# A two-layer attention and expert kernel: twelve early tiles, a slot for each hop of the tail, and half of the first weights fetched at an earlier step

## The chip, the cores and the metric

The kernel runs on one core of a Trainium2 chip. Its engines are the tensor engine (PE, matmuls; PEld loads their weights), the vector engine (DVE), ScalarE (ACT), GpSimd (POOL) and SyncE (SP, which here issues most DMAs). The metric is device time of one launch in microseconds: the median of 3 runs is 1725.58 (1724.13 to 1726.16).

## The reference, cut to what matters

32 sequences of 128 tokens, width 256, 16 heads of 16. Four residual steps follow each other; in the second and fourth each token goes to two of eight experts. `_layernorm`, `softmax` and the rest are the usual ones.

```python
x = x + tanh(g_xattn[0]) * xattn0(layernorm(x), ctx)      # W_Q, W_K, W_V, W_O with biases, softmax over all keys
x = x + tanh(g_ffn[0])   * moe0(layernorm(x))             # top 2 of 8, relu, hidden 1024, gate = softmax of two logits
x = x + tanh(g_xattn[1]) * xattn1(layernorm(x), ctx)      # no output product, causal and key mask
x = x + tanh(g_ffn[1])   * moe1(layernorm(x))             # top 2 of 8, silu(x@w_gate) * (x@w_up) @ w_down, hidden 512
```

## The kernel before, in words

Both layers have the same plan: an attention loop and then a loop over expert tiles. All matmuls are in float32r, and precision is kept by splitting each operand into a high part (rounded by ScalarE) and a low part (the rest, by the vector engine or POOL): three products stand for one (`three`, L443 to 446).

Attention runs over steps s from -8 to 127 (`pe_step`, `act_step`, `dve_step`, `pool_step`, each engine with its own list of what it does in a step). A step handles four heads of a batch; four steps are one of the 32 batches, four batches are a group g, eight groups in all. After a batch's heads come its output transposes (`ot`), output product (`op`, layer 0 alone), residual update (`xup`) and statistics. After a group's four batches come its normalised rows (`xr`), their transposes (`lt`), router logits (`lg`), selection of two experts, ranks among the tokens of each expert (`rk`), row numbers (PI) and eight scatters by POOL that put each row into a table in DRAM sorted by expert (L1525). `Part` (L113) gives the step of each of these by group.

The expert loop takes NT = 39 tiles of 256 rows of that table. A tile's rows are fetched by SP (`sp_fetch_x`, L1606), transposed on the tensor engine (`pe_turn_x`, L614), multiplied up in four quarters (`pe_up`) while the tile before is multiplied down in two halves (`pe_down`). Its weights come in four parts n = 0 to 3 (L1582): ScalarE makes the high part (`act_w`, L840), and the low part is made by POOL (n = 0 and 3) or the vector engine (n = 1 and 2) in `low_w` (L1384). The tensor engine's first quarter of tile i waits for the low part n = 0 of tile i. POOL also scatters each finished tile's result (`pool_y`).

The two loops overlap. The last steps of attention (s = 128 to 149, LAST = 150) stand among the first tiles, four to a tile: `late(i, k)` gives step 128 + 4i + k for slot k of tile i. On the tensor engine the slots stand after the second and the fourth quarter up and after each half down (in tile 0 after each quarter); on the others after the second hidden quarter, the fourth, and around the copies of weights; POOL does slot 0 before its result scatter, slot 1 after it, slots 2 and 3 after the low weights n = 0. Every engine works strictly in its written order, so an operation that waits in a slot holds all behind it. PSUM's last two banks are dealt in turn to transposes, logits, ranks and output products in the order of the tensor engine's list (`uses_bk`), each use waiting until the one two before it has been read.

The first KE = 8 tiles are known to be full once group 4 has been counted (`dve_lists_early`, steps 101 to 104). The other tiles need the final counts (`dve_lists`, from step LIST1 = 147). SP's loop over i fetches rows for tile i + 2 at its head, but those of tile KE at the end of pass i = KE - 2, after all scatters and eight pad writes (`pad`, L833) have landed; the pads are issued in the same pass.

Of the kernel before, what the change touches and what calls it, by code (L numbers as in the profile page):

```python
# [19 lines left out]
NG = B // G  # L20
# [3 lines left out]
GE, KE = 5, 8  # L24
# [104 lines left out]
FIRST, START, LAST = -8, 128, 150  # L129
LIST0, TX, LIST1 = 101, (124, 126), 147  # L130
# [14 lines left out]
def bat(s, k):  # L145
    b, m = divmod(s - k, 4)
    return b if m == 0 and 0 <= b < B else None

# [7 lines left out]
def program(nc, A):  # L156
    ctx = ExitStack()
    with ctx:  # L158
# [216 lines left out]
        def uses_step(L, s, out):  # L375
                for name, at, empty in (("xt", X0, v_xt), ("q", Q0, v_q), ("k", K0, v_k), ("v", V0, a_v)):
                    for n in range(2):
                        if (g := grp(s, at[n])) is not None:
                            out.append(((name, g, n), empty[L, g, n]))
                if L == 0 and s == 1:  # L380
                    out.append((("bo", 0), s_bov[0]))
                if L == 0 and (b := bat(s, 8)) is not None:
                    out.append((("ot", b), v_ot[b]))
                if L == 0 and (b := bat(s, 10)) is not None:
                    out.append((("op", b), v_xup[0, b]))
                for p in PARTS:
                    for t in range(2):
                        if s == p.lt[t]:
                            out.append((("lt", p.key, t), a_lt[(L,) + p.key + (t,)]))
                    if s == p.e1:  # L390
# [125 lines left out]
        def pe_step(e, w, L, s):  # L516
# [43 lines left out]
            if L == 0 and (b := bat(s, 8)) is not None:  # L560
# [5 lines left out]
            if L == 0 and (b := bat(s, 10)) is not None:  # L566
                w.wait_ge(*v_ot[b])
                w.wait_ge(*s_wl[0, 3])
                bank_free(w, L, "op", b)
                for t in range(2):  # L570
                    ins = three(e, place[0, "op", b][:, 0:D], (OT[:, b % 2, 0, t, :], OT[:, b % 2, 1, t, :]), (WR[:, 3, 0, t], WR[:, 3, 1, t]), t == 0, t == 1)
                ins.then_inc(*m_op(b))
            for p in PARTS:
# [8 lines left out]
                if s == p.e1:  # L582
# [184 lines left out]
        def act_step(e, w, L, s):  # L767
# [13 lines left out]
            if 0 <= s < NU:  # L781
                i = s
# [10 lines left out]
            if L == 0 and (b := bat(s, 8)) is not None:  # L793
# [4 lines left out]
            for p in PARTS:  # L798
                k, g, js = (L,) + p.key, p.g, p.js
                for t in range(2):  # L800
                    if s == p.lt[t]:
# [5 lines left out]
                if s == p.lt[1]:  # L807
# [183 lines left out]
        def dve_rests(e, w, L, s):  # L991
# [5 lines left out]
            if L == 0 and (b := bat(s, 8)) is not None:  # L997
# [3 lines left out]
            if L == 0 and (b := bat(s, 10)) is not None:  # L1001
# [3 lines left out]
            for p in PARTS:  # L1005
                if s == p.e1:
# [8 lines left out]
                if s == p.rk:  # L1015
# [183 lines left out]
        def dve_step(e, w, L, s):  # L1199
# [20 lines left out]
            dve_rests(e, w, L, s - 1)  # L1220
            for j in range(G):
# [21 lines left out]
            for p in PARTS:  # L1243
                k = (L,) + p.key
                if s == p.e0:
                    dve_rsqrt_start(e, w, 1, p.js).then_inc(*v_rs2(*k))
                if s in (p.e0 + 2, p.e0 + 3):
# [8 lines left out]
                    for j in (range(p.lo, mid), range(mid, p.hi))[s - p.e0 - 2]:  # L1256
                        ins = e.tensor_scalar(xr(p.g)[:, 0, j, 0:D], X[:, p.g * G + j], mv[:, 1, j, 0:1], rs[:, 1, 1, j:j + 1], ALU.subtract, ALU.mult)
                    if s == p.e0 + 3:
# [21 lines left out]
            if (b := bat(s, 12)) is not None:  # L1280
# [215 lines left out]
        def pool_step(e, w, L, s):  # L1496
# [10 lines left out]
            for p in PARTS:  # L1507
                k, g = (L,) + p.key, p.g
                if s == p.e0:
                    w.wait_ge(*v_rs2[k])  # L1510
                    rsqrt_steps(e, w, p_c, 1, p.js, (0, 1, 2)).then_inc(*p_rs2(*k))
                if s == p.e0 + (4 if g < NG - 1 else 0):
# [7 lines left out]
                for n, (z, j) in enumerate((z, j) for z in range(2) for j in range(p.lo, p.hi)):  # L1520
                    if s == p.scatter + n // 2:
# [148 lines left out]
        def sp_attention(e, w, L):  # L1670
            sp_first(e, w, L)
            for s in range(FIRST, START):
# [139 lines left out]
```

## Time and profile before

| | |
|---|---|
| median of 3 runs | 1725.58 us |
| profiled execution | 1727.66 us, span 1725.9 us |
| TensorE clock granted, mean | 0.958 of full speed |
| busy in the span | PE 91%, PEld 82%, ACT 71%, DVE 69%, POOL 48% |
| idle before PE's row transposes, for a fetch (L614) | 30.3 us |
| fetch of 512 KB weights, issue to landing | 4.9 us |
| HBM, mean | 139 GB/s |

Busy shares are averages over stages with different limits, so the stages have to be read apart: attention of layer 0 ends near 357 us and that of layer 1 near 1278 us, and each is followed by the tiles of its layer. In the rows below a number in square brackets is the idle time of the engine before the instruction, with what ended it; "issue" is a wait that the profile puts down to nothing.

### The profile page before, as it was taken

To read this page: it belongs to the slowest core of one execution; us is meant where nothing else is said; L and a number is where in the kernel's file an instruction comes from. 1 tells how busy PE (TensorE), PEld (TensorE's weight loads), DVE (VectorE), ACT (ScalarE), POOL (GpSimd) and SP (SyncE) were. 2 spreads that over 40 slices of the span, in tenths; PEclk is the share of its full clock that TensorE was granted. 3 is DMA by queue.
4 is the path that set the end of the run, shared out by engine and by line. 5 is a ranking of instruction groups with operands and counts; after the bars stand their busy time and mean duration, and the time that the engine had idled before them with its cause. 6 is when DMAs were issued, how large, how long until landed. Compare 5 with 4: busy or idle time off the path is not lost. (4 is left out here: it accounts for less than half of the span.)

```text
span 1725.9 us, 37428 instructions
## 1 busy us (share of the span) xinstructions
PE 1562.6 (91%) x12728; PEld 1419.0 (82%) x12728; DVE 1187.1 (69%) x2778; ACT 1233.7 (71%) x2854; POOL 832.5 (48%) x907
## 2 busy tenths in 40 slices
PE   7999999978859999999998999999886749999997
PEld 5788888767859999999996777777776749999996
DVE  5677777747637677777866788888766626666664
ACT  5888888856637788888863877777775527777774
POOL 4124444336445556565553113333335546777775
PEclk9999999988979999999998999999998869999998
DMA  3222222245577777777742233333244567887883
GB/s 109 54 52 74 73 74 74 54 120 175 161 205 232 225 233 227 227 234 235 223 153 79 71 82 101 104 105 103 58 123 135 147 172 198 237 228 222 231 239 97
DMA packets 208990, 256.57 MB, mean 149 GB/s; under 512 B 29555, under 2 KB 156788, under 8 KB 208800
## 3 DMA queue, kind: packets, MB, share of 16 engines
q1 hardware_dynamic: 187040, 219.53, 43.7%
q0 software_dynamic: 21120, 34.39, 7.6%
q8 instruction: 101, 1.65, 0.4%
q14 instruction: 89, 0.73, 0.1%
q10 hardware_dynamic: 640, 0.26, 0.1%
HBM read 194.54 MB, written 45.74 MB: 139 GB/s over the span
## 5 line engine op out<-in xcount | busy, mean ns | idle before, releaser
L1384 POOL TENSOR_TENSOR KXR<-U,KXR 128x1024 fp32r<-128x1024 f32 (+1 forms) x156 | 350.0, 2245 | 308.0 <-ACT KXR L840 301.3
L444 PE MATMUL ps<-QR,KXR 128*128 128x256 f32 x1248 | 368.9, 296 | 32.3 <-issue 29.9
L445 PE MATMUL ps<-QR,KXR 128*128 128x256 f32 x1248 | 360.9, 289 | 0.0
L446 PE MATMUL ps<-QR,KXR 128*128 128x256 f32 x1248 | 360.8, 289 | 0.0
L840 ACT ACTIVATE KXR<-U 128x1024 fp32r<-128x1024 f32 (+1 forms) x312 | 288.0, 947 | 78.4 <-PE ps L446 50.6
L779 ACT ACTIVATE U<-ps,mx 128x128 f32<-128x128 f32 x1024 | 298.0, 403 | 21.5 <-DVE mx L1205 21.5
L444 PEld LDWEIGHTS ps<-QR,KXR 128*128 128x128 f32 x1248 | 248.0, 199 | 34.6 <-issue 31.5
L445 PEld LDWEIGHTS ps<-QR,KXR 128*128 128x128 f32 x1248 | 248.0, 199 | 0.0
L446 PEld LDWEIGHTS ps<-QR,KXR 128*128 128x128 f32 x1248 | 247.3, 198 | 0.0
L1205 DVE TENSOR_REDUCE mx<-ps 128x4 f32<-128x512 f32 x256 | 174.3, 684 | 68.2 <-PE ps L446 35.8
L1384 DVE TENSOR_TENSOR KXR<-U,KXR 128x1024 fp32r<-128x1024 f32 (+1 forms) x156 | 173.2, 1146 | 35.1 <-ACT KXR L840 34.9
L870 ACT ACTIVATE U<-ps,b1s 128x256 f32<-128x256 f32 x312 | 130.1, 471 | 61.1 <-PE ps L446 61.0
L522 PE MATMUL ps<-cst,U 128*128 128x128 f32 x1024 | 164.0, 283 | 10.5 <-DVE U L1215 10.0
L786 ACT ACTIVATE U<-ps 128x512 f32<-128x512 f32 x256 | 166.0, 648 | 7.1 <-PE ps L522 7.0
L1525 POOL DMA_INDIRECT xs_scr<-XR,PI x112 | 111.0, 991 | 110.8 <-DVE PI L1114 82.1
L522 PEld LDWEIGHTS ps<-cst,U 128*128 128x128 f32 x1024 | 118.1, 143 | 47.8 <-issue 23.0
L1417 DVE TENSOR_TENSOR PTR<-U,PTR 128x512 fp32r<-128x512 f32 x80 | 97.1, 1244 | 79.8 <-ACT PTR L881 79.6
L444 PE MATMUL ps<-KXR,PTR 128*128 128x256 f32 x480 | 137.8, 287 | 7.8 <-POOL KXR L1384 5.4
L445 PE MATMUL ps<-KXR,PTR 128*128 128x256 f32 x480 | 137.0, 285 | 0.0
L446 PE MATMUL ps<-KXR,PTR 128*128 128x256 f32 x480 | 136.9, 285 | 0.0
L1552 POOL DMA_INDIRECT out<-U,xi x78 | 121.7, 1561 | 20.0 <-issue 19.7
L1426 DVE TENSOR_TENSOR ps<-U,ps 128x256 f32<-128x256 f32 x156 | 70.3, 450 | 88.3 <-ACT U L873 87.8
(228 smaller groups left out, 4034.2 us busy)
## 6 DMA issues: line engine op xcount, KB each, us to landing
U<-in_wpack SPq DMA_DIRECT2D x234, 512.0 KB, 4.9
U<-in_wpack SPq DMA_DIRECT2D x78, 256.0 KB, 4.4
KXR<-U SPq DMA_DIRECT2D x504, 32.0 KB
U<-xs_scr SPq DMA_DIRECT2D x39, 258.0 KB, 4.6
U<-xs_scr SPq DMA_DIRECT2D x39, 257.0 KB, 4.7
U<-in_ctx_t SPq DMA_DIRECT2D x16, 512.0 KB, 5.7
U<-ys_scr SPq DMA_DIRECT2D x32, 256.0 KB, 3.4
U<-in_L_ffn_b SPq DMA_DIRECT2D x39, 128.0 KB, 4.0
```

The source lines that it names most:

```text
L444: e.matmul(o, wh, xh, start=first, stop=False)
L445: e.matmul(o, wh, xl, start=False, stop=False)
L446: return e.matmul(o, wl, xh, start=False, stop=done)
L522: ins = e.transpose(bank[:, h * 128:(h + 1) * 128], PB[:, i % 3, h], ident)
L779: ins = e.activation(PB[:, i % 3, h], SB_[i % 3][:, h * 128:(h + 1) * 128], ACT.Exp, bias=mx[:, i % 4, h:h + 1], scale=-1.0)
L786: e.activation(PT[:, i % 3].rearrange("p h k -> p (h k)"), pt_place["p", i][:, :], ACT.Copy).then_inc(*a_pt(L, i))
L840: e.activation(w_cols(L, WH, n), w_raw(L, n), ACT.Copy).then_inc(*a_w[n](L, i))
L870: ins = e.activation(HB[:, r, f], HBK[q][:, z * 256:z * 256 + 256], ACT.Relu, bias=b1s[:, r, f:f + 1])
L1205: e.tensor_reduce(mx[:, i % 4], SB_[i % 3][:, :].rearrange("p (h k) -> p h k", h=4), AX.X, ALU.min).then_inc(*v_mx(L, i))
L1384: e.tensor_tensor(w_cols(L, WL, n), w_raw(L, n), hi, ALU.subtract).then_inc(*l_w[n](L, i))
L1525: e.indirect_dma_start(xs_d[L], bass.IndirectOffsetOnAxis(ap=PI[:, g % 2, z, j:j + 1], axis=0), xr(g)[:, z, j, 0:ROWS[L]], None).then_inc( ...
L1552: ins = e.indirect_dma_start(ys_d[1], at, yo[:, r, a, :], None, bounds_check=T - 1, oob_is_err=False, compute_op=ALU.add)
```

## The change

KE becomes 12 and LAST 162, LIST1 158; the pads move to pass KE - 3 of SP's loop. `Part` no longer has two rhythms but one table for groups 0 to 5 (the same steps as before) and one for groups 6 and 7, whose operations each get a step of their own, also apart on the engines: transposes on the tensor engine (`lt`) and the copies of their results on ScalarE (`alt`) are one step apart, logits and their copy, ranks and their copy likewise. Group 6 is normalised at steps 130 and 131 in place of 123 and 124, scattered from 146 in place of 130; group 7 is normalised at 144 and 145 in place of 139 and 140, scattered from 158 in place of 146. The output steps of batches 30 and 31 are spread by LATE_AT. ScalarE copies tile 0's first two weight parts at steps 124 and 125 in place of 124 and 126. SP fetches the rows of tiles 0 and 1 at step 112 in place of 117, and tile 0's weight parts 0 and 1 at 112 in place of 121.

```diff
-GE, KE = 5, 8
+GE, KE = 5, 12
-FIRST, START, LAST = -8, 128, 150
-LIST0, TX, LIST1 = 101, (124, 126), 147
+FIRST, START, LAST = -8, 128, 162
+LIST0, TX, LIST1 = 101, (124, 126), 158
...
-        self.e0 = 16 * g + 4 * hi + 9
-        fast = g >= NG - 2
-        self.lt = (self.e0 + 4, self.e0 + 5)
-        self.e1 = self.e0 + 6
-        (self.max, self.index, self.sel, self.gates, self.exp, self.gates2, self.rk, self.rank, self.rows, self.scatter) = (
-            self.e1 + k for k in ((1, 1, 1, 1, 1, 2, 2, 3, 3, 3) if fast else (1, 2, 2, 3, 3, 4, 3, 4, 5, 6)))
+        if g < NG - 2:
...
+        else:
+            last = g == NG - 1
+            e = START + (16 if last else 2)
+            self.start, self.root = (e - 3, e - 2) if last else (START - 7, START - 7)
+            self.x, self.tok, self.lt, self.alt, self.axr = (e, e + 1), e + (0 if last else 2), (e + 2 + 2 * (not last), e + 3 + 2 * (not last)), (e + 3 + 2 * (not last), e + 4 + 2 * (not last)), e + 5 + 2 * (not last)
+            e = self.axr + 1
+            self.lg, self.vlg, self.max, self.index, self.sel, self.gates = e, e + 1, e + 1, e + 2, e + 2, e + 3
+            self.rk, self.exp, self.gates2, self.vrk, self.rank, self.rows = e + 4, e + 4, e + 5, e + 5, e + 6, e + 7
+            self.scatter = [e + 8 + (n // 2 if last else n) for n in range(8)]
...
+AT = {"ot": 8, "a_ot": 8, "v_ot": 9, "op": 10, "xup": 11, "stats": 12}
+LATE_AT = {"ot": {30: 0, 31: 5}, "a_ot": {30: 1, 31: 6}, "v_ot": {30: 2, 31: 7}, "op": {30: 4, 31: 8}, "xup": {30: 5, 31: 9},
+           "stats": {28: 4, 29: 5, 30: 6, 31: 10}}
...
+def step(s, name):
+    for b in range(B):
+        if s == (START + LATE_AT[name][b] if b in LATE_AT[name] else 4 * b + AT[name]):
+            return b
+    return None
...
-                    if s == p.lt[t]:
+                    if s == p.alt[t]:
...
+                    if s == TX[0] + i:
+                        act_w(e, w, L, 0, i)
                     if s == TX[i]:
-                        act_w(e, w, L, 0, i)
                         act_turn_x(e, w, L, i)
...
-                if s == 117:
+                if s == 112:
                     for i in range(2):
                         sp_fetch_x(e, w, L, i)
-                if s == 121:
-                    for b in (B - 2, B - 1):
-                        w.wait_ge(*d_k[key_queue(L, b)][L, b, 7])
-                    v = sp_expert(e, w, L, 0)
-                    for n in range(4):
-                        sp_fetch(e, w, L, 0, n, v)
+                for s0, b0, n0 in ((112, B - 6, 0), (121, B - 2, 2)):
+                    if s == s0:
+                        for b in (b0, b0 + 1):
+                            w.wait_ge(*d_k[key_queue(L, b)][L, b, 7])
+                        v = sp_expert(e, w, L, 0)
+                        for n in (n0, n0 + 1):
+                            sp_fetch(e, w, L, 0, n, v)
...
-                if i == KE - 2:
+                if i == KE - 3:
                     for x in range(E):
                         pad(e, w, L, x)
```

The order in which the instructions stand on the tensor engine at the end of layer 0's attention, before: sums of a batch's heads (L512), transposes of fetched rows (cst,U at L614), probabilities (L522), group 6's rows (cst,XR), outputs (OS), output product (WR,OT) and group 6's logits (rw,U).

```order
L512 MATMUL ps<-U,VA 32x128 x8
L614 MATMUL ps<-cst,U 128x128 x4
L522 MATMUL ps<-cst,U 128x128 x4
L580 MATMUL ps<-cst,XR 128x128 x4
L522 MATMUL ps<-cst,U 128x128 x4
L547 MATMUL ps<-cst,OS 128x128 x4
```

Then, past the output product's six matmuls:

```order
L580 MATMUL ps<-cst,XR 128x128 x4
L512 MATMUL ps<-U,VA 32x128 x8
L614 MATMUL ps<-cst,U 128x128 x4
L522 MATMUL ps<-cst,U 128x128 x4
L588 MATMUL ps<-rw,U 128x8 x8
L444 MATMUL ps<-QR,KXR 128x256
```

After the change, the same place:

```order
L537 MATMUL ps<-U,VA 32x128 x8
L639 MATMUL ps<-cst,U 128x128 x4
L547 MATMUL ps<-cst,U 128x128 x8
L572 MATMUL ps<-cst,OS 128x128 x4
L469 MATMUL ps<-WR,OT 128x256
L470 MATMUL ps<-WR,OT 128x256
```

and past the output product:

```order
L471 MATMUL ps<-WR,OT 128x256
L537 MATMUL ps<-U,VA 32x128 x8
L639 MATMUL ps<-cst,U 128x128 x4
L547 MATMUL ps<-cst,U 128x128 x4
L469 MATMUL ps<-QR,KXR 128x256
```

Group 6's two sets of transposes and its logits are gone from this place, and the first product of tile 0 (QR,KXR) follows the probabilities; the logits and transposes stand in tiles 1 and 2.

On POOL, in layer 0, around the scatters of group 7 (xs_scr<-U), before: low weights n = 0 (2x512) and n = 3 (1024), results (ys_scr).

```order
L1384 TENSOR_TENSOR KXR<-U,KXR 128x2x512
L1525 DMA xs_scr<-U,PI 34816x257 x4
L1384 TENSOR_TENSOR KXR<-U,KXR 128x1024
L1525 DMA xs_scr<-U,PI 34816x257 x2
L1550 DMA ys_scr<-U,xi 8192x256 x2
L1525 DMA xs_scr<-U,PI 34816x257 x2
L1384 TENSOR_TENSOR KXR<-U,KXR 128x2x512
```

After the change:

```order
L1414 TENSOR_TENSOR KXR<-U,KXR 128x2x512
L1555 DMA xs_scr<-U,PI 34816x257 x4
L1414 TENSOR_TENSOR KXR<-U,KXR 128x1024
L1555 DMA xs_scr<-U,PI 34816x257 x2
L1580 DMA ys_scr<-U,xi 8192x256 x2
L1555 DMA xs_scr<-U,PI 34816x257 x2
L1414 TENSOR_TENSOR KXR<-U,KXR 128x2x512
```

The pattern is the same, four scatters behind one tile's low weights n = 0, then two and two around the results of the next; it stands before the low weights n = 0 of tile 9 in place of tile 6.

On SP, in layer 0, around the last pad write (xs_scr<-cst), before: what follows is biases (b1s).

```order
L832 TENSOR_LOAD pdi
L832 ISA x2
L833 ISA
L833 DMA xs_scr<-cst 128x2x257
L1576 TENSOR_LOAD tvi
L1576 ISA x2
L1587 ISA
L1587 DMA b1s<-in_wpack 128x8
```

After the change:

```order
L858 TENSOR_LOAD pdi
L858 ISA x2
L859 ISA
L859 DMA xs_scr<-cst 128x2x257
L1635 TENSOR_LOAD tvi
L1635 ISA x2
L1636 ISA
L1636 DMA U<-xs_scr 128x2x257
```

Behind the pads there now stands a fetch of rows (U<-xs_scr), that of tile 11.

## Rows read from the trace of the kernel before

**Rows 1.** Busy time by stretch: start:end, length, engines' busy us, clock, DMA.

```profile
354.00:391.00 37.00, 24.16 (x190) 21.70 (x179) 16.77 (x55) 17.36 (x38) 9.16 (x15) 0.83 0.33 108
391.00:484.00 93.00, 70.81 (x542) 69.52 (x541) 59.94 (x124) 56.03 (x96) 54.95 (x48) 0.90 0.54 164
1278.00:1305.00 27.00, 17.94 (x150) 16.05 (x139) 16.19 (x59) 15.98 (x29) 5.92 (x9) 0.85 0.28 93
1305.00:1392.00 87.00, 58.62 (x412) 56.58 (x410) 55.23 (x166) 42.09 (x88) 51.81 (x48) 0.81 0.52 149
```

**Rows 2.** Time line of PE, layer 0: start, us, line, operation, [idle before].

```profile
356.71 0.66 PE L614 MATMUL ps<-cst,U 128*128 128x128 f32 x4
362.05 1.09 PE L580 MATMUL ps<-cst,XR 128*128 128x128 f32 x4 [4.24 <-DVE OT L1000]
...
370.98 0.63 PE L614 MATMUL ps<-cst,U 128*128 128x128 f32 x4 [4.37 <-DVE X L1004]
...
391.22 1.04 PE L614 MATMUL ps<-cst,U 128*128 128x128 f32 x4
...
436.21 0.90 PE L580 MATMUL ps<-cst,U 128*128 128x128 f32 x4 [2.67 <-DVE U L1257]
...
456.87 0.58 PE L594 MATMUL ps<-SEL,cst 128*128 128x32 f32 x2 [4.37 <-DVE SEL L1042]
...
484.21 0.55 PE L444 MATMUL ps<-QR,KXR 128*128 128x256 f32 x1 [7.00 <-issue]
...
509.53 1.12 PE L614 MATMUL ps<-cst,U 128*128 128x128 f32 x4 [12.09 <-DMA U<-xs_scr]
...
523.97 0.60 PE L614 MATMUL ps<-cst,U 128*128 128x128 f32 x4
...
535.87 0.60 PE L614 MATMUL ps<-cst,U 128*128 128x128 f32 x4
...
635.01 0.60 PE L614 MATMUL ps<-cst,U 128*128 128x128 f32 x4
```

**Rows 3.** Time line of PE, layer 1.

```profile
1278.17 0.66 PE L614 MATMUL ps<-cst,U 128*128 128x128 f32 x4
...
1304.68 1.05 PE L614 MATMUL ps<-cst,U 128*128 128x128 f32 x4
...
1392.49 0.55 PE L444 MATMUL ps<-QR,KXR 128*128 128x256 f32 x1 [7.86 <-issue]
...
1428.72 0.60 PE L614 MATMUL ps<-cst,U 128*128 128x128 f32 x4
...
1437.80 0.60 PE L614 MATMUL ps<-cst,U 128*128 128x128 f32 x4
```

**Rows 4.** Time lines of ACT and DVE: undisturbed tile, then ranks.

```profile
640.62 0.63 ACT L881 ACTIVATE WR<-U 128x512 fp32r<-128x512 f32 x1
...
641.28 3.23 DVE L1417 TENSOR_TENSOR WR<-U,WR 128x512 fp32r<-128x512 f32 x1 [1.07 <-ACT WR L881]
...
645.63 2.35 DVE L1384 TENSOR_TENSOR KXR<-U,KXR 128x1024 fp32r<-128x1024 f32 x2
...
462.45 0.76 DVE L1098 TENSOR_TENSOR CR<-CR,RK 128x8 f32<-128x8 f32 x4
```

**Rows 5.** Time line of POOL around group 7's scatters, layer 0.

```profile
464.74 1.71 POOL L1525 DMA_INDIRECT xs_scr<-U,PI  x1 [10.42 <-DVE PI L1114]
...
481.76 4.66 POOL L1384 TENSOR_TENSOR KXR<-U,KXR 128x1024 fp32r<-128x1024 f32 x2
```

**Rows 6.** Time line of SP's queue; last, the page's DMA issues.

```profile
330.44 14.81 SPq L740 DMA_DIRECT2D KXR<-U  x16
...
487.14 9.55 SPq L833 DMA_DIRECT2D xs_scr<-cst  x8
...
637.46 0.38 SPq L1606 DMA_DIRECT2D U<-xs_scr  x1
...
U<-xs_scr SPq DMA_DIRECT2D x39, 257.0 KB, 4.7
```

More of the change, by code:

```diff
@@ L118, in __init__ @@
         self.js, self.bs = slice(lo, hi), slice(g * G + lo, g * G + hi)
-        self.e0 = 16 * g + 4 * hi + 9
-        fast = g >= NG - 2
-        self.lt = (self.e0 + 4, self.e0 + 5)
-        self.e1 = self.e0 + 6
-        (self.max, self.index, self.sel, self.gates, self.exp, self.gates2, self.rk, self.rank, self.rows, self.scatter) = (
-            self.e1 + k for k in ((1, 1, 1, 1, 1, 2, 2, 3, 3, 3) if fast else (1, 2, 2, 3, 3, 4, 3, 4, 5, 6)))
+        if g < NG - 2:
+            e = 16 * g + 4 * hi + 9
+            self.start, self.root, self.x, self.tok = e, e, (e + 2, e + 3), e + 4
+            self.lt, self.alt, self.axr = (e + 4, e + 5), (e + 4, e + 5), e + 5
+            self.lg, self.vlg, self.max, self.index, self.sel, self.gates = e + 6, e + 7, e + 7, e + 8, e + 8, e + 9
+            self.rk, self.exp, self.gates2, self.vrk, self.rank, self.rows = e + 9, e + 9, e + 10, e + 10, e + 10, e + 11
+            self.scatter = [e + 12 + n // 2 for n in range(8)]
+        else:
[7 more added lines that the diff above has]
+            self.scatter = [e + 8 + (n // 2 if last else n) for n in range(8)]
 PARTS = [Part(g, 0, G) for g in range(NG)]
 NU = 4 * B
-FIRST, START, LAST = -8, 128, 150
-LIST0, TX, LIST1 = 101, (124, 126), 147
 X0, Q0, K0, V0 = (6, 7), (8, 9), (0, 1), (10, 11)
@@ L381, in uses_step @@
                     out.append((("bo", 0), s_bov[0]))
-                if L == 0 and (b := bat(s, 8)) is not None:
+                if L == 0 and (b := step(s, "ot")) is not None:
                     out.append((("ot", b), v_ot[b]))
-                if L == 0 and (b := bat(s, 10)) is not None:
+                if L == 0 and (b := step(s, "op")) is not None:
                     out.append((("op", b), v_xup[0, b]))
@@ L559, in pe_step @@
                 ins.then_inc(*s_bomm(0))
-            if L == 0 and (b := bat(s, 8)) is not None:
+            if L == 0 and (b := step(s, "ot")) is not None:
                 w.wait_ge(*v_on[0, b])
@@ L565, in pe_step @@
                 ins.then_inc(*m_ot(b))
-            if L == 0 and (b := bat(s, 10)) is not None:
+            if L == 0 and (b := step(s, "op")) is not None:
                 w.wait_ge(*v_ot[b])
@@ L792, in act_step @@
                         take(e, w, L, g, n)
-            if L == 0 and (b := bat(s, 8)) is not None:
+            if L == 0 and (b := step(s, "a_ot")) is not None:
                 w.wait_ge(*m_ot[b])
@@ L996, in dve_rests, with dve_small @@
                         rest(e, w, L, g, n)
-            if L == 0 and (b := bat(s, 8)) is not None:
+        def dve_small(e, w, L, s):
+            if L == 0 and (b := step(s, "v_ot")) is not None:
                 w.wait_ge(*a_ot[b])
@@ L1000, in dve_rests @@
                 e.tensor_tensor(ol, place[0, "ot", b][:, 0:256], oh.bitcast(F32), ALU.subtract).then_inc(*v_ot(b))
-            if L == 0 and (b := bat(s, 10)) is not None:
+            if L == 0 and (b := step(s, "xup")) is not None:
                 w.wait_ge(*m_op[b])
@@ L1244, in dve_step @@
                 k = (L,) + p.key
-                if s == p.e0:
+                if s == p.start:
                     dve_rsqrt_start(e, w, 1, p.js).then_inc(*v_rs2(*k))
-                if s in (p.e0 + 2, p.e0 + 3):
+                if s in p.x:
                     w.wait_ge(*p_rs2[k])
@@ L1255, in dve_step @@
                     mid = (p.lo + p.hi) // 2
-                    for j in (range(p.lo, mid), range(mid, p.hi))[s - p.e0 - 2]:
+                    for j in (range(p.lo, mid), range(mid, p.hi))[s - p.x[0]]:
                         ins = e.tensor_scalar(xr(p.g)[:, 0, j, 0:D], X[:, p.g * G + j], mv[:, 1, j, 0:1], rs[:, 1, 1, j:j + 1], ALU.subtract, ALU.mult)
-                    if s == p.e0 + 3:
+                    if s == p.x[1]:
                         ins.then_inc(*v_xr(*k))
@@ L1279, in dve_step @@
                     dve_lists(e, w, L, n)
-            if (b := bat(s, 12)) is not None:
+            if (b := step(s, "stats")) is not None:
                 w.wait_ge(*v_xup[L, b])
@@ L1520, in pool_step @@
                 for n, (z, j) in enumerate((z, j) for z in range(2) for j in range(p.lo, p.hi)):
-                    if s == p.scatter + n // 2:
+                    if s == p.scatter[n]:
                         w.wait_ge(*v_pi[k])
```

15 lines of the change are left out of this document (8 added, 7 removed).

## The prediction

> **What bounds the kernel now.** I first read busy and granted clock by stage [rows 1], then the tensor engine's line in time through the tail of each layer [rows 2, 3], then one undisturbed tile on the two engines that feed it [rows 4], then POOL's and SP's queues [rows 5, 6]. The reader is to see four things.
>
> In undisturbed tiles the tensor engine never waits: a tile takes 11.9 us in layer 0 (523.97 to 535.87) and 9.08 in layer 1 (1428.72 to 1437.80) [rows 2, 3]. So time can only come back from the stretch around the seam, where attention ends and expert tiles begin. There the engine is busy 24.2 of 37 us, then 70.8 of 93, in layer 1 17.9 of 27, then 58.6 of 87, and its granted clock is 0.81 to 0.90 of full speed: after an idle stretch the lower level of 1.2 GHz is granted for a while, so most waits cost 1 to 2 us more than their length [rows 1]. The waits have names: 4.24 us for a bank behind the vector engine, 4.37 for a residual update, 2.67 for a normalised row, 4.37 for the selection, 7.00 before tile 6, 12.09 for the first row fetch that needs the final lists [rows 2].
>
> The 7.00 is POOL's: it issues eight scatters of the last group from 464.74, puts other work between, and only then makes the low part of tile 6's first weights (first of the two at 481.76, so about 484.1); the tensor engine starts at 484.21 [rows 2, 5]. The 12.09 is SP's: eight pad writes take 9.55 us of issuing, and the row fetch stands behind them [rows 6].
>
> **The change part by part.** I cut each layer into A (first transposes of gathered rows to the start of tile 1), B (from there to the last wait on POOL's scatters) and C (to the first undisturbed tile).
>
> *A, hops of group 6 out of attention and tile 0.* Group 6's normalisation, transposes, logits and ranks leave steps 123 to 130, and batch 30's output product leaves tile 0. Today A is 34.5 us in layer 0 (356.71 to 391.22) and 26.5 in layer 1 (1278.17 to 1304.68) [rows 2, 3]. The 4.24 us wait goes, since the vector engine no longer sits on group 5's last scatter before it frees the bank; the 4.37 goes, since half of tile 0's weights are there early and the residual update is no longer queued behind the copy of group 6's rows. What is left: busy 24.2 at clock 0.83 is about 20.1 at full clock; the 32 of 190 matmuls that leave (8 transposes, 16 logits, 6 output products, 2 ranks) are 3.8 us at 0.12 each, and 2.7 lie before the cut [rows 1, 2]. That makes 13.6, and I add 3 for steps that stay paced by ScalarE: 16.6. Layer 1: 17.9 at 0.85 is 15.2, less 26 matmuls (3.1), plus 3: 15.1 [rows 1]. Gain 17.9 and 11.4, together 29.3. The bounds are the 3 us (0 if nothing paces the steps, 9 if as much idle stays as in layer 1 today).
>
> The earlier fetch of half the weights costs SP's queue: two row fetches and two 512 KB fetches now stand between the key copies of batches 30 and 31. Those 16 copies take SP from 330.44 to 345.25 [rows 6], and the tensor engine goes on without an idle row after them. Bounds: nothing, to 4 us a layer (the 4.7 us in which a row fetch lands, less what is over when batch 31's copies are issued [rows 6]). I take 1.5 each, nearer to nothing since eight copies are issued over some 5 us: A gains 26.3 net. The Trainium skill, "DMA: Bandwidth & Descriptors", section "Queues, rings and completion order", says that on each DMA engine the descriptors of a ring are consumed in ring order; by that the keys wait for all the weights in front of them, 4 us a layer, and the sum below is 5 us less gain. No run here shows yet which.
>
> *B, a slot per hop.* A slot is reached by each engine at its own time. In a tile of layer 0 the tensor engine is at its four slots 3.3, 6.2, 9.0 and 11.9 us after the tile's start (quarters of 96 matmuls). ScalarE reaches its first at 6.2 (640.62 + 0.63 against 635.01), the vector engine at 9.5 (641.28 + 3.23), about 10.7, 11.8 and 13.0 (645.63 + 2.35) [rows 2, 4]. So a vector result from slot 0 or 1 of a tile is late for tensor slot 2, however tidy the table looks. Layer 0, by the new table: tile 1, output and transposes behind the vector engine's slots 1 and 3, 3.8 in four waits; tile 2, the output product of batch 31 at tensor slot 0 wants a bank that ScalarE frees in its own slot 0 (6.2 + 0.6 against 3.3), 3.5; tile 3, ranks behind the selection, 1.5 (4.37 today, one slot further now); tile 4, transposes of group 7 at slot 2 behind normalisation at vector slots 0 and 1, where some fifteen small operations of 0.2 now stand in front (0.76 for four), 4.0: between the 2.67 of today's hop and 6; tile 6, ranks, 1.5. Then tile 9: the last group's rows are found at vector slot 1 of tile 7, 13 us in, POOL needs 19.4 from its first scatter to the end of the next low weights (464.74 to 481.76 + 2.33), which is 20.6 us into tile 8 and 8.3 too late [rows 2, 4, 5]. Waits 22.6, work that moved in or stays 9.9, clock 3.5: 36.0. Today B is 391.22 to 484.21 less five tiles of 11.9 and 0.4: 33.1. In layer 1 the tile is 2.8 us shorter and POOL's work is not: 1.6 in tile 1, 7.3 in tile 4, 2 each before tiles 7 and 8, 11.7 before tile 9, 7.9 of work, 5 of clock, 37.5; today 1304.68 to 1392.49 less 45.8: 42.0 [rows 3]. B loses 2.9 and gains 4.5: 1.6 gained. Every wait here is off by up to 2 either way: bounds 15 us more or less over both layers.
>
> The skill's page "SBUF — State Buffer", section "Who interferes with whom", says that a vector instruction with two SBUF inputs blocks against a GpSimd instruction that reads SBUF. Here one such operation takes 3.23 us, while the low products, twice as large, take 2.35 for two [rows 4]; if POOL's new place in tile 4 spares it, the vector slots come 2.5 us earlier, and the sum gains that much a layer.
>
> *C, twelve early tiles.* The twelfth tile's rows are again fetched at the end of an SP pass (i = 10), and the pads moved one pass ahead, to i = 9, in front of tile 11's rows. In an undisturbed tile that fetch is issued 2.45 us in (637.46) and lands 4.7 later, 4.8 us before it is needed [rows 2, 6]. With the pads in front (first 2.9 us after tile 9's first matmul as today, 9.55 long, 1.2 to the fetch, 4.7 to land) it lands 18.3 us in, needed at 11.5: a wait of 6.8. Then tile 12's fetch, last in its pass, lands about 7.3 us after tile 11 should start, 8.3 with the pass still late. With 2.5 of clock (14.44 for the tile after today's wait) C costs 17.6; today 484.21 to 523.97 less 23.5 is 16.3. Layer 1 the same way, with 2.8 us less to hide in: 9.6 + 8.2 + 2.5 = 20.3 against 1392.49 to 1428.72 less 17.8: 18.4 [rows 2, 3, 6]. C loses 3.2. So the twelve early tiles buy nothing of themselves: the wait is split into two.
>
> Sum: 26.3 + 1.6 - 3.2 = 24.7 us. The profiled execution took 1727.66 (span 1725.9); 1703.0 by that, and the median of the runs lies 2.1 lower: 1701.
>
> **The rivals.** First, the hops really vanish: B's new waits fall to a third because POOL, late in every tail tile, no longer blocks the vector engine, and the pads run while the tensor engine waits for POOL. Then B gives back 25 more: 1676. For it: 37.5 us of layer 1's A and B are idle today [rows 1], so there is room. Against: the slot times of rows 4.
>
> Second, the waits only change places: A's waits reappear in tiles 1 to 4, since the same chain of vector, ScalarE and tensor operations is as long as before and other engines keep their order. Gain 4 at most: 1722. Against: 8.6 us of waits in layer 0's A hang on one scatter and one weight copy that leave the path.
>
> Third, slower: C comes at full price twice. If the second fetch waits as long as the first does today (12 in layer 0, 14 in layer 1 in place of 8) and each tile between must also wait for its weights behind the pads, C costs 17 more a layer, 34 in all, and the gain is gone: 1718 with one layer so, 1735 with both. It decides when SP, held by POOL's late weights before tile 9, starts the pads more than 5 us into that tile. For it: SP issues in order, and tile 10's weights do wait for POOL. Against: today's pads start 2.9 us in, in the same position.
>
> **How the numbers follow.** Forecast 0.60, first rival 0.18, second 0.11, third 0.11. Of a change under 0.2% (3.5 us) a measurement of this kernel tells nothing, so faster is below 1722, slower above 1729. Of the second half lies within, with a little from the forecast's tail; of the third most is slower: faster 0.83, within 0.08, slower 0.09. The forecast's own bounds (A 0 to 9 a layer where I took 3, keys 0 to 4, B 15 either way, all at once being unlikely) give 1684 to 1719; the range reaches into the first and second rivals, 1677 to 1724.
>
> **What would show it.** Tile 1 of layer 0 starting 15 to 19 us after its first gathered transposes (34.5 today) shows A. Waits of 3 to 4 us in tile 2 on ScalarE, in tile 4 on the vector engine, and of 6 to 10 before tile 9 on POOL's low weights show B. Two waits for fetched rows, before tiles 10 and 11, of 5 to 10 each, show C. I am wrong if only one fetch wait is left, if B's waits are below 10 us a layer, or if batch 31's scores wait more than 4 us for their keys.

## The result, and the profile after

The changed kernel takes 1708.57 us (median of 4 runs, 1705.51 to 1712.26), the kernel before 1724.86 beside it: a ratio of 0.9906, 95% interval 0.9885 to 0.9928. Forecast were 1701 and a range of 1677 to 1724. The profiled execution spans 1707.3 us, 18.6 less than before.

The stretches first, as in [rows 1]: A (first row transposes to tile 1) and B (to the last wait for POOL's scatters) of layer 0, the same of layer 1, then C of both. Columns as there.

```profile
355.00:374.00 19.00, 14.94 (x165) 13.09 (x158) 9.98 (x15) 15.14 (x35) 7.79 (x10) 1.00 0.37 111
374.00:508.00 134.00, 111.78 (x873) 110.36 (x871) 96.78 (x195) 87.63 (x151) 80.97 (x64) 0.92 0.61 179
1267.00:1283.00 16.00, 12.89 (x134) 11.19 (x135) 9.20 (x19) 13.04 (x30) 7.22 (x14) 1.00 0.31 94
1283.00:1397.00 114.00, 87.94 (x674) 85.83 (x673) 84.55 (x247) 67.83 (x140) 76.48 (x64) 0.90 0.64 169
508.00:562.50 54.50, 41.06 (x297) 40.69 (x298) 25.06 (x28) 28.30 (x50) 21.39 (x13) 0.84 0.75 201
1396.70:1445.70 49.00, 34.58 (x225) 34.19 (x226) 16.18 (x38) 19.49 (x42) 20.26 (x12) 0.77 0.68 175
```

A now runs at the full granted clock (0.83 and 0.85 in [rows 1]); C runs at 0.84 and 0.77. The tensor engine's line in time shows where the stretches begin and end, and the waits that answer to those of [rows 2] (layer 0) and [rows 3] (layer 1):

```profile
349.27 0.50 PE L469 MATMUL ps<-KXR,QR 128*128 128x512 f32 x1 [1.06 <-DMA KXR<-U]
357.92 0.66 PE L639 MATMUL ps<-cst,U 128*128 128x128 f32 x4
373.66 0.60 PE L639 MATMUL ps<-cst,U 128*128 128x128 f32 x4
...
443.74 1.12 PE L605 MATMUL ps<-cst,U 128*128 128x128 f32 x4 [5.16 <-DVE U L1287]
508.14 0.55 PE L469 MATMUL ps<-QR,KXR 128*128 128x256 f32 x1 [6.58 <-issue]
527.20 1.12 PE L639 MATMUL ps<-cst,U 128*128 128x128 f32 x4 [5.84 <-DMA U<-xs_scr]
548.87 1.12 PE L639 MATMUL ps<-cst,U 128*128 128x128 f32 x4 [7.45 <-DMA U<-xs_scr]
562.48 0.60 PE L639 MATMUL ps<-cst,U 128*128 128x128 f32 x4
...
1269.47 0.66 PE L639 MATMUL ps<-cst,U 128*128 128x128 f32 x4
1283.32 0.60 PE L639 MATMUL ps<-cst,U 128*128 128x128 f32 x4
1334.87 1.12 PE L605 MATMUL ps<-cst,U 128*128 128x128 f32 x4 [7.39 <-DVE U L1287]
1396.72 0.55 PE L469 MATMUL ps<-QR,KXR 128*128 128x256 f32 x1 [9.24 <-issue]
1414.73 1.12 PE L639 MATMUL ps<-cst,U 128*128 128x128 f32 x4 [6.67 <-DMA U<-xs_scr]
1433.84 1.12 PE L639 MATMUL ps<-cst,U 128*128 128x128 f32 x4 [7.74 <-DMA U<-xs_scr]
1445.65 0.60 PE L639 MATMUL ps<-cst,U 128*128 128x128 f32 x4
```

Layer 1 of the kernel before has one long fetch wait, as layer 0 has its 12.09 in [rows 2]:

```profile
1416.94 1.12 PE L614 MATMUL ps<-cst,U 128*128 128x128 f32 x4 [14.21 <-DMA U<-xs_scr]
```

This one wait of 12.09 (14.21 in layer 1) has become two, 5.84 and 7.45 (6.67 and 7.74), and POOL's low weights are waited for in front of tile 9 in place of tile 6. SP's queue shows the two fetches, as [rows 6] did the one: the pads stand ahead of tile 11's rows (521.53), and tile 12's rows come last in the next pass (545.12, with tile 13's behind them).

```profile
497.66 12.65 SPq L1612 DMA_DIRECT2D U<-in_wpack  x4
511.08 9.63 SPq L859 DMA_DIRECT2D xs_scr<-cst  x8
521.53 0.40 SPq L1636 DMA_DIRECT2D U<-xs_scr  x1
...
545.12 1.59 SPq L1636 DMA_DIRECT2D U<-xs_scr  x2
```

The first row holds the finding that the experiment with early pads rests on: its four issues take under 0.4 us each, and some 10 of its 12.65 us, up to the second issue at 508.22, are SP's wait for POOL's low weights of tile 9.

By the prediction's own cuts (A; B less its tiles; C less its tiles; us, layer 0 / layer 1):

| | before | forecast | after |
|---|---|---|---|
| A | 34.5 / 26.5 | 16.6 / 15.1 | 15.7 / 13.9 |
| B | 33.1 / 42.0 | 36.0 / 37.5 | 38.9 / 40.4 |
| C | 16.3 / 18.4 | 17.6 / 20.3 | 18.9 / 22.0 |

B after is 508.14 - 373.66 less eight tiles of 11.9 and 0.4, and 1396.72 - 1283.32 less eight of 9.08 and 0.4; C is 562.48 - 508.14 less 35.4 for three tiles, and 1445.65 - 1396.72 less 26.9. The cuts hold 21.0 us of the gain; 2.4 are lost outside them (A begins 1.2 us later in layer 0), which leaves the 18.6 of the spans.

### The profile page after: what moved, and what is told of

Its sections match the earlier page's. It is cut to its first block and busy times, and to the rows that moved or that the text cites. A ratio compares the mean times of both kernels' runs of the same rounds, so it can differ in the third digit from the quotient of the medians.

```text
span 1707.3 us, 37441 instructions
## 1 busy us (share of the span) xinstructions
PE 1557.3 (91%) x12728; PEld 1413.8 (83%) x12728; DVE 1196.3 (70%) x2778; ACT 1233.1 (72%) x2854; POOL 842.3 (49%) x907
## 3 DMA queue, kind: packets, MB, share of 16 engines
q8 instruction: 101, 1.65, 0.4%
## 5 line engine op out<-in xcount | busy, mean ns | idle before, releaser
L1414 POOL TENSOR_TENSOR KXR<-U,KXR 128x1024 fp32r<-128x1024 f32 (+1 forms) x156 | 354.8, 2275 | 303.2 <-ACT KXR L866 302.9
L469 PE MATMUL ps<-QR,KXR 128*128 128x256 f32 x1248 | 368.1, 295 | 22.4 <-issue 16.1
L804 ACT ACTIVATE U<-ps,mx 128x128 f32<-128x128 f32 x1024 | 298.4, 405 | 17.9 <-DVE mx L1234 17.9
L469 PEld LDWEIGHTS ps<-QR,KXR 128*128 128x128 f32 x1248 | 247.5, 198 | 24.7 <-issue 17.6
L469 PE MATMUL ps<-KXR,WR 128*128 128x256 f32 x456 | 130.8, 287 | 3.4 <-DVE U L1441 2.0
```

What stands on the lines that cost most here:

```text
L469: e.matmul(o, wh, xh, start=first, stop=False)
L804: ins = e.activation(PB[:, i % 3, h], SB_[i % 3][:, h * 128:(h + 1) * 128], ACT.Exp, bias=mx[:, i % 4, h:h + 1], scale=-1.0)
L1414: e.tensor_tensor(w_cols(L, WL, n), w_raw(L, n), hi, ALU.subtract).then_inc(*l_w[n](L, i))
```

## The experiments

All ratios are to the kernel before, run beside each, with a 95% interval. A, B and C are by the cuts above; each profile is one execution, and kernels that are the same in A differ there by up to 1.6 us (15.7 to 17.3 in layer 0).

**Twelve early tiles alone, on the kernel before.**

```diff
-GE, KE = 5, 8
+GE, KE = 5, 12
```

> The kernel before with KE = 12 in place of 8 and nothing else: pads at the head of pass 10, tile 12's rows fetched at its end. Theory: twelve early tiles buy nothing of themselves, since the wait is for eight pad writes and a fetch behind them in SP's queue and not for the final lists; the waits of 12.1 and 14.2 us reappear four tiles later: within 4 us of the kernel before. Rival: with the lists known for four tiles the pads pass early or beside other waits, and the time falls by 10 us or more.

1727.77 us, 1.0016 (1.0004 to 1.0029). The waits stand four tiles later at their full price; tensor engine, layer 0 and layer 1:

```profile
560.28 1.12 PE L614 MATMUL ps<-cst,U 128*128 128x128 f32 x4 [12.34 <-DMA U<-xs_scr]
...
1455.74 1.12 PE L614 MATMUL ps<-cst,U 128*128 128x128 f32 x4 [13.77 <-DMA U<-xs_scr]
```

The time is within the theory's 4 us: early tiles alone gain nothing.

**The early fetch undone.**

```diff
-                if s == 112:
+                if s == 117:
                     for i in range(2):
                         sp_fetch_x(e, w, L, i)
-                for s0, b0, n0 in ((112, B - 6, 0), (121, B - 2, 2)):
+                for s0, b0, n0 in ((121, B - 2, 0), (121, B - 2, 2)):
```

> The changed kernel with the early fetch alone undone: rows of tiles 0 and 1 fetched at step 117, tile 0's weight parts 0 and 1 at step 121, as before. Theory: the early fetch itself is worth little; it costs batch 31's keys 1.1 us (layer 0) and about 1.6 (layer 1), and saves tile 0 a wait for its weights; within 4 us of the changed kernel's 1708.6, and the 1.06 us wait for the keys at the end of layer 0's attention gone. Rival: A's gain of 19 and 13 us hangs on the weights being there; then the stretch from the first gathered transposes to tile 1 grows by 4 us or more in each layer and the time is above 1716.

1709.64 us, 0.9914 (0.9892 to 0.9936): no difference from the change that these runs can tell. A is 17.3 (358.95 to 376.26) and 13.9, so the rival falls. The keys are waited for here too (0.58 us), so that part of the theory isn't borne out. ScalarE's copies of these weights stay at their new steps. Its layer 0 holds the third rival's price in one place: the second fetch is waited for 12.10 us.

**Tile 11's rows ahead of the pads.**

```diff
-                if i == KE - 3:
-                    for x in range(E):
-                        pad(e, w, L, x)
...
                     sp_fetch_x(e, w, L, i + 2)
+                if i == KE - 3:
+                    for x in range(E):
+                        pad(e, w, L, x)
```

> The changed kernel with one swap on SP: in pass 9 the row fetch of tile 11 is issued ahead of the eight pad writes instead of behind them. Theory: the wait of tile 10's start for that fetch (5.84 and 6.67 us) goes, with 1 to 3 us of clock each; the second wait (7.45 and 7.74) stays within 2 us: 1692 to 1697. Rival: the wait is only pushed to the second fetch, which grows by what the first loses; then the time stays within 3 us of 1708.6.

1705.50 us, 0.9884 (0.9861 to 0.9907). Tensor engine, layer 0 and the second fetch of layer 1:

```profile
535.98 0.36 PE L469 MATMUL ps<-KXR,WR 128*128 128x256 f32 x1 [4.30 <-POOL KXR L1414]
549.99 1.11 PE L639 MATMUL ps<-cst,U 128*128 128x128 f32 x4 [9.43 <-DMA U<-xs_scr]
...
1434.54 1.12 PE L639 MATMUL ps<-cst,U 128*128 128x128 f32 x4 [13.90 <-DMA U<-xs_scr]
```

The rival's mechanism holds, though the time lies 0.1 us outside its range: the first fetch wait is gone, the second grew by 1.98 in layer 0 and by 6.16 in layer 1 (7.45 to 9.43, 7.74 to 13.90), and the weights behind the pads are late as well (4.30). Changing the order inside the queue doesn't shorten the queue.

**The pads where SP waits.**

```diff
-                if i == KE - 3:
-                    for x in range(E):
-                        pad(e, w, L, x)
...
-                if i + 2 < NT and i + 2 != KE:
+                if i + 2 < NT:
                     sp_fetch_x(e, w, L, i + 2)
...
+                if i == KE - 4:
+                    for x in range(E):
+                        pad(e, w, L, x)
                 if i + 2 < NT:
                     v = sp_expert(e, w, L, i + 2)
...
-                if i + 2 == KE:
-                    sp_fetch_x(e, w, L, KE)
```

> The changed kernel with the eight pad writes moved into the 9.5 us (layer 0) and 10.8 us (layer 1) in pass 8 in which SP waits for POOL's low weights of tile 9, and tile 12's rows fetched at the head of pass 10 like those of any other tile. The row numbers that the pads need are there 8 us before (DVE, 490.0 us in layer 0). Theory: both waits for row fetches go (13.3 and 14.4 us) with most of the slow clock behind them (5.5 and 7.6): 1668 to 1682. Rival: the fetch is not the only thing late there; the weights that SP issues after the pads become the wait, and the tail keeps half of these waits: 1690 to 1700.

1672.33 us, 0.9694 (0.9674 to 0.9715): 36 us less than the change, as the theory had it, and both waits are gone. SP's queue, then the tensor engine in layer 0 (layer 1: no fetch wait at tiles 10 and 11 either):

```profile
496.43 10.04 SPq L859 DMA_DIRECT2D xs_scr<-cst  x8
507.24 2.19 SPq L1612 DMA_DIRECT2D U<-in_wpack  x3
```

```profile
505.71 0.55 PE L469 MATMUL ps<-QR,KXR 128*128 128x256 f32 x1 [5.07 <-issue]
519.62 0.66 PE L639 MATMUL ps<-cst,U 128*128 128x128 f32 x4
531.58 0.60 PE L639 MATMUL ps<-cst,U 128*128 128x128 f32 x4
```

The pads take as long as before (10.04 us), but now inside SP's wait for POOL; tile 10 and tile 11 start without a wait, and a tile takes 11.96.

**The same on the kernel before, in pass 5.**

The same edit with the numbers of that kernel; the pads stand ahead of the fetches of the pass that wait for POOL, and tile 8's rows are fetched at the head of pass 6.

```diff
-                if i == KE - 2:
-                    for x in range(E):
-                        pad(e, w, L, x)
...
+                if i == KE - 3:
+                    for x in range(E):
+                        pad(e, w, L, x)
                 if i + 2 < NT:
                     v = sp_expert(e, w, L, i + 2)
```

> The kernel before (eight early tiles, all its steps) with the pad writes in pass 5, in the 11 us in which SP waits for POOL's low weights of tile 6 (473.2 to 484.3 in layer 0), and tile 8's rows fetched at the head of pass 6. Theory: what bound the start of tile 7 was the pads' place in SP's queue; the waits of 12.1 and 14.2 us go, with some 4 us of clock: 1692 to 1700, without any other part of the change. Rival: with eight early tiles the lists come too late for that place and SP is held, so half or more of the waits stays: 1706 or more.

1696.47 us, 0.9831 (0.9806 to 0.9856). Eight early tiles are enough for it: the tensor engine waits for POOL in front of tile 6 as before, and for no fetch in tiles 7 to 10 (layer 0; the same in layer 1).

```profile
485.15 0.55 PE L444 MATMUL ps<-QR,KXR 128*128 128x256 f32 x1 [7.05 <-issue]
498.47 0.60 PE L614 MATMUL ps<-cst,U 128*128 128x128 f32 x4
```

Moving the eight pad writes, and with them one row fetch, gives more (28 us) than the whole change (16).

**Group 6 back.**

```diff
-        if g < NG - 2:
+        if g == NG - 2:
+            e = 16 * g + 4 * hi + 9
+            self.start, self.root, self.x, self.tok = e, e, (e + 2, e + 3), e + 4
+            self.lt, self.alt, self.axr = (e + 4, e + 5), (e + 4, e + 5), e + 5
...
+        elif g < NG - 2:
```

> The changed kernel with group 6 alone put back to its steps of before (normalised at 123 and 124, scattered from 130, close hops); the rest of the change stays. Theory: A's gain comes from group 6's hops leaving attention and tile 0, so the stretch from the first gathered transposes to tile 1 goes from 15.7 back to 28 to 34 us in layer 0 and from 13.9 to 22 to 26 in layer 1; tiles 1 to 3 give back some 4 us a layer: 1718 to 1728. Rival: A's gain comes from the earlier weights and the spread output product of batch 30, and group 6 only changes its place: 1706 to 1712.

1704.63 us, 0.9884 (0.9863 to 0.9905): not slower than the change. Tensor engine, the ends of A and B in both layers:

```profile
356.54 0.66 PE L647 MATMUL ps<-cst,U 128*128 128x128 f32 x4
380.12 0.63 PE L647 MATMUL ps<-cst,U 128*128 128x128 f32 x4 [1.22 <-DVE OT L1037]
501.78 0.55 PE L477 MATMUL ps<-QR,KXR 128*128 128x256 f32 x1 [6.57 <-issue]
...
1264.89 0.66 PE L647 MATMUL ps<-cst,U 128*128 128x128 f32 x4
1288.10 1.05 PE L647 MATMUL ps<-cst,U 128*128 128x128 f32 x4
1394.21 0.55 PE L477 MATMUL ps<-QR,KXR 128*128 128x256 f32 x1 [9.30 <-issue]
```

A is 7.9 and 9.3 us longer than after the change (23.6 and 23.2), B 12.8 and 7.3 shorter (26.1 and 33.1). Group 6's hops out of A cost in B what they save: the theory's 1718 to 1728 falls, the time lies just below the rival's 1706 to 1712, and both movements are there.

**Group 6 back and the last outputs close.** The last kernel, and in `step`:

```diff
-        if s == (START + LATE_AT[name][b] if b in LATE_AT[name] else 4 * b + AT[name]):
+        if s == (4 * b + AT[name]):
```

> The changed kernel with group 6 back at its steps (1704.6 us) and the outputs, residual updates and statistics of batches 28 to 31 back at their close steps too; group 7's table, twelve tiles and the early fetch stay. Theory: what still shortened the stretch from the first gathered transposes to tile 1 in that run (23.6 us in layer 0 against 34.5 before) is the spread of batch 30's output and of the statistics; it goes back to 30 us or more in layer 0 and hardly changes in layer 1, which has no output product: 1709 to 1716. Rival: it is group 7's table that clears the vector engine there, and the stretch stays under 26 us: 1702 to 1708.

1703.68 us, 0.9894 (0.9868 to 0.9919). A is 24.7 and 23.2, B 22.2 and 33.2. My theory falls: the outputs' spread isn't what shortens A, and it buys nothing. Time and stretch are the rival's; its reason, group 7's table, is put to the test next.

**Group 7's table, twelve tiles and early pads alone.** The last kernel with the pads in pass 8, and with the first fetches and copies of weights as before:

```diff
-                if s == 112:
+                if s == 117:
                     for i in range(2):
                         sp_fetch_x(e, w, L, i)
-                for s0, b0, n0 in ((112, B - 6, 0), (121, B - 2, 2)):
+                for s0, b0, n0 in ((121, B - 2, 0), (121, B - 2, 2)):
...
-                    if s == TX[0] + i:
-                        act_w(e, w, L, 0, i)
                     if s == TX[i]:
+                        act_w(e, w, L, 0, i)
```

> The kernel with the pads in pass 8 (1672.3 us), with everything else of the change undone but group 7's table and the twelve tiles: group 6 and the outputs of the last batches at their steps of before, rows and weights of the first tiles fetched and copied as before. Theory: group 6's move and the earlier weights each clear the same wait ahead of the first transposes of tile 1 (4.37 us in layer 0), so either alone could be undone freely, but not both: the stretch to tile 1 goes from 24.7 back to 33 to 35 us in layer 0 and from 23.2 to 26 in layer 1, and some of it comes back in tiles 1 to 3: 1676 to 1686. Rival: group 7's statistics leaving attention cleared it; the stretch stays under 27 and 24 us, and the time is 1668 to 1674.

1680.71 us, 0.9738 (0.9721 to 0.9754), within the theory's range. Tensor engine, A of layer 0:

```profile
355.95 0.66 PE L647 MATMUL ps<-cst,U 128*128 128x128 f32 x4
360.86 0.63 PE L613 MATMUL ps<-cst,XR 128*128 128x128 f32 x4 [3.81 <-DVE OT L1036]
369.55 1.09 PE L647 MATMUL ps<-cst,U 128*128 128x128 f32 x4 [3.93 <-DVE X L1040]
389.29 0.60 PE L647 MATMUL ps<-cst,U 128*128 128x128 f32 x4
```

The two waits of [rows 2] are back (3.81 and 3.93 for 4.24 and 4.37), A is 33.3 and 26.4. So group 7's table by itself doesn't clear them. With group 6 in attention the earlier weights (fetch and copies together) do; with group 6 in the tiles the earlier fetch isn't needed, as the run without it shows. Whether the earlier copies are needed there was not tried.

**Early pads with group 6 back.** The diffs of these two experiments together.

> The kernel with the pads in pass 8 (1672.3 us) and group 6 put back to its steps of before, as in the run that did this alone (1704.6 against 1708.6). Theory: group 6's slots only carry the waits of its hops from the stretch before tile 1 (7.9 and 9.4 us there) into tiles 1 to 9 (12.8 and 7.3), so the 4 us come back here too: 1666 to 1670. Rival: that difference hung on the two fetch waits, which grew and shrank with it; then no difference: 1671 to 1675.

1670.79 us, 0.9677 (0.9652 to 0.9702). Theory and rival lie 4 us apart, and the runs spread over 7 (1667.61 to 1674.61): not decided. It, the early pads alone (1672.33) and the split pads below (1671.03) are the fastest versions here; all three beat both kernels.

**Scatters behind tile 9's low weights, with early pads.**

```diff
-FIRST, START, LAST = -8, 128, 162
+FIRST, START, LAST = -8, 128, 164
...
-            self.scatter = [e + 8 + (n // 2 if last else n) for n in range(8)]
+            self.scatter = [e + 8 + (n // 2 + 2 * (n // 4) if last else n) for n in range(8)]
```

> The kernel with the pads in pass 8 (1672.3 us), and POOL's last four scatters of group 7 two steps later (162 and 163), so that they stand behind the low weights of tile 9 in place of ahead of them. Theory: the wait in front of tile 9 (5.07 and 8.75 us in that kernel) is POOL's queue alone; four scatters of 1.28 us with their gaps leave it, so it falls by 5 in each layer, with 1 of clock: 1659 to 1664. Rival: POOL's low weights then wait for the finished tile's result, and less than half of it comes back: 1667 to 1672.

1676.11 us, 0.9705 (0.9678 to 0.9732): no gain. Tensor engine, layer 0, then layer 1:

```profile
505.49 0.35 PE L469 MATMUL ps<-QR,KXR 128*128 128x256 f32 x1 [0.97 <-issue]
525.59 1.11 PE L639 MATMUL ps<-cst,U 128*128 128x128 f32 x4 [8.35 <-DMA U<-xs_scr]
...
1379.45 0.55 PE L469 MATMUL ps<-QR,KXR 128*128 128x256 f32 x1 [2.99 <-issue]
1395.45 1.11 PE L639 MATMUL ps<-cst,U 128*128 128x128 f32 x4 [4.76 <-DMA U<-xs_scr]
```

The theory's wait did fall (5.07 to 0.97, 8.75 to 2.99), but neither theory nor rival saw the rest: the pads had been hidden in that very wait, and now tile 11's rows stand behind the pads and are waited for (8.35, 4.76).

**The pads split, four in pass 8 and four in pass 9.**

```diff
-                if i == KE - 4:
-                    for x in range(E):
-                        pad(e, w, L, x)
+                if i in (KE - 4, KE - 3):
+                    for x in range(E // 2):
+                        pad(e, w, L, x + (i - (KE - 4)) * E // 2)
```

> The kernel with the last four scatters behind tile 9's low weights (1676.1 us), with the eight pad writes split: four in pass 8 and four in pass 9, each ahead of the weight fetches that wait for POOL. Theory: in that run the wait before tile 9 did fall (5.07 to 0.97 and 8.75 to 2.99), but the pads had been hidden in this very wait, and tile 11's row fetch behind them was then 8.35 and 4.76 us late; four pads a pass find cover, so that fetch wait goes: 1659 to 1666. Rival: tile 12's fetch, which needs all pads landed, or the weights behind the pads become late in its place: 1669 to 1677.

1671.03 us, 0.9692 (0.9661 to 0.9723). The 8.35 is 1.35 now, but 2.49 us appear at tile 11 for a fetch in layer 0 and 1.91 behind the start of tile 10 in layer 1: the rival's time. What SP has to issue in these passes no longer finds 10 free us.

**Group 7's later hops two slots later, thirteen tiles.** The kernel with split pads, and:

```diff
-GE, KE = 5, 12
+GE, KE = 5, 13
-FIRST, START, LAST = -8, 128, 164
-LIST0, TX, LIST1 = 101, (124, 126), 158
+FIRST, START, LAST = -8, 128, 168
+LIST0, TX, LIST1 = 101, (124, 126), 160
...
-(e + 2 + 2 * (not last), e + 3 + 2 * (not last)), (e + 3 + 2 * (not last), e + 4 + 2 * (not last)), e + 5 + 2 * (not last)
+(e + 4, e + 5), (e + 5, e + 6), e + 7
...
-            self.scatter = [e + 8 + (n // 2 + 2 * (n // 4) if last else n) for n in range(8)]
+            self.scatter = [e + 10 + n // 2 + 2 * (n // 4) if last else e + 8 + n for n in range(8)]
```

> The kernel with split pads, with group 7's hops from its transposes on two steps later (148 in place of 146), its scatters at 162, 163, 166 and 167, lists from 160, thirteen early tiles, pads in passes 9 and 10. Theory: the wait in tile 4 for the vector engine's normalised rows (5.2 to 5.8 us in layer 0, 7.4 to 8.3 in layer 1) is a slot set too early, so it goes but for 2 us, with 1 to 2 of clock, and nothing behind is on a path: 12 us less than with split pads alone. Rival: as with group 6 the wait moves along to the later hops (ranks, the low weights behind the scatters), and less than 4 us come back.

1677.64 us, 0.9728 (0.9711 to 0.9745): slower than the split pads by their medians. The wait in tile 4 falls to 2.40 in layer 0 and goes in layer 1; in layer 1 there come others, the tensor engine's sums by releaser (us in total, times, longest) from 1256 to 1416 being:

```profile
PE ps L639 <- DMA U<-xs_scr: 7.9, 5, 3.2
PE ps L469 <- DVE KXR L1414: 5.4, 3, 2.4
PE ps L469 <- issue: 3.8, 1, 3.8
```

As with group 6, the wait moves along, as the rival had it: fetches, the vector engine and POOL are each waited for 2 to 4 us at a time.

## Why the prediction was right, and where its steps were off

The sign and the range hold; the gain was put at 24.7 us, and the spans differ by 18.6 (the medians by 16.3). By parts, forecast and measured: A 29.3 and 31.4, what lies outside the cuts -3.0 (the keys) and -2.4, B 1.6 and -4.2, C -3.2 and -6.2.

*A* came as forecast: 18.8 and 12.6 us saved against 17.9 and 11.4, and full clock. Five later versions with the same A save 17.2 to 17.3 and 11.1 to 11.2. The keys were waited for 1.06 us in layer 0, and 0.42 to 2.56 in the versions with the same fetch (in layer 1 not at all after the change), not 4, so the rule that a ring's descriptors are consumed in order (the Trainium skill, "DMA: Bandwidth & Descriptors", "Queues, rings and completion order") did not cost the 4 us that I worked out from it.

But the step's reason was half right. I gave the gain to group 6's hops, and the 4.37 us wait to the weights. A and B together, from the profiles:

| kernel | A, layer 0 / 1 | B, layer 0 / 1 | sum |
|---|---|---|---|
| before | 34.5 / 26.5 | 33.1 / 42.0 | 136.1 |
| group 7's table and twelve tiles | 33.3 / 26.4 | 22.2 / 32.9 | 114.8 |
| and earlier weights | 24.7 / 23.2 | 22.2 / 33.2 | 103.3 |
| and outputs spread | 23.6 / 23.2 | 26.1 / 33.1 | 106.0 |
| and group 6's slots (the change) | 15.7 / 13.9 | 38.9 / 40.4 | 108.9 |

The second row's kernel has its pads early as well; early pads alone change B little (36.7 and 40.4 for 38.9 and 40.4). Each row is one profile, so differences of 2 or 3 us are not told apart; the large ones are. Group 7's table gives 21 us, 20 of them in B (with twelve tiles alone there is no gain), the earlier weights 11 to 12 in A, and group 6's slots take 17 us out of A, add 20 to B and gain nothing. So the second rival (waits only change places) is right for group 6 and wrong for group 7.

*B* is the step that failed: "1.6 gained" was 4.2 lost. Its waits were sized well in sum: 22.6 us forecast for layer 0, 22.4 measured (1.00, 2.66, 3.32, 1.65, 5.16, 1.98, 6.58), 24.6 and 25.8 in layer 1. That the sums agree so well is in part luck, since single waits missed and made up for each other: the 1.5 of tile 6 didn't come and 1.98 in tile 8 did; before tile 9 layer 1 waits 9.24 where 11.7 were put. What was too small is the rest, moved work and slow clock: 13.4 forecast and 16.5 measured, 12.9 and 14.6. Of the two it is the clock, by an estimate from the rows of B above: 0.08 of 111.78 busy us and 0.10 of 87.94 are some 9 us a layer, where 3.5 and 5 were put, and what is left for the moved work is less than forecast. (The same estimate is a little high for C: 6.6 and 8.0 for the 5.6 and 7.6 below.)

*C* was forecast to lose 3.2 and lost 6.2. The two waits are there, at 5.84 and 7.45 for 6.8 and 8.3 (6.67 and 7.74 for 9.6 and 8.2). Again the rest was too small: 2.5 a layer for the clock, where 5.6 and 7.6 are left. The 2.5 is the price of one tile behind one wait, and C has three such tiles, behind 6.58, 5.84 and 7.45 in layer 0: they are 1.6, 2.3 and 1.7 us longer than an undisturbed one (2.6, 2.3 and 2.7 in layer 1), at mean granted clocks of 0.84 and 0.77. The kernel before has two, and there too more than 2.5 is left: 16.3 - 12.09 and 18.4 - 14.21, 4.2 in each layer.

The first rival (B's waits fall to a third) is refuted by the 22.4 us; the third (C at full price twice) by C. Its sign, pads started more than 5 us into tile 9, didn't come either: they start 2.9 us behind that tile's first product (511.08 - 508.14). Still, four versions of the change wait 11.30 to 13.90 us for the second fetch in one of their layers (12.10 with the late fetch). "The twelve early tiles buy nothing of themselves" is shown by the run that has them alone. What the prediction did not ask is whether the pads' place was the cause of both fetch waits; that was worth 36 us, twice the change.

Every version waits for a row fetch once more in layer 0, at the start of tile KE + 3 (2.31 us at tile 15 after the change, 2.03 at tile 11 before). SP's queue shows what stands ahead of it. After the change, in pass 14, SP first issues three weight matrices and two blocks of context for layer 1's attention (from 588.24), and the row fetch comes at 592.23, 5.9 us into the tile, where the two passes ahead of it have theirs at 1.8 and 2.4. Layer 1 of these two kernels has no such issues and no wait there. No version moved them, so this is read from the queue and not tested.

Open: which of the three fastest versions is the fastest.

## What to carry to other kernels

When a queue's late transfer is the bound, look in the same queue for a wait that comes earlier and is long enough to hold the work in front of it; that was worth more than a new order for all engines. A hop moved out of one stage is to be judged by the sum of that stage and those that receive it. And work hidden in a wait is in the way as soon as that wait is shortened: cover has to be counted again after each edit.

## What the runs showed of the hardware

Operations of 0.17 us on the vector engine took 3 us. The four additions in the ranks (CR, RK) take 0.76 us together in [rows 4]; after the change they take 3.67 in tile 4 of layer 0, 3.07 of it one addition, ahead of the normalised rows for which the tensor engine waits 5.16. Vector engine and POOL there, and the same in layer 1 with another small operation:

```profile
436.38 3.67 DVE L1127 TENSOR_TENSOR CR<-CR,RK 128x8 f32<-128x8 f32 x4
...
1329.87 3.29 DVE L1132 TENSOR_TENSOR PX<-RK,CR 128x32 f32<-128x32 f32 x1
```

```profile
437.18 2.43 POOL L1414 TENSOR_TENSOR KXR<-U,KXR 128x1024 fp32r<-128x1024 f32 x1
...
1330.17 2.94 POOL L1414 TENSOR_TENSOR KXR<-U,KXR 128x1024 fp32r<-128x1024 f32 x1
```

The long addition ends at 436.57 + 3.07 = 439.64 and the other operation at 1329.87 + 3.29 = 1333.16, just behind POOL's low product (437.18 + 2.43 = 439.61, 1330.17 + 2.94 = 1333.11). In all seven kernels with group 6's slots one addition takes 3.09 us or more; in the seven without them none takes more than 0.20. This agrees with the Trainium skill's page "SBUF — State Buffer", section "Who interferes with whom": a vector instruction with two SBUF inputs contends with a GpSimd instruction that reads SBUF. The prediction had used that rule for a gain; here it may be some 3 us of each tile 4 wait, an estimate from 3.67 - 0.76 that no run tests apart.
